# A masked feed-forward kernel: last two batches kept on chip, weight rounding dealt out anew, every second unit in three passes

## The reference, cut to what matters

```python
def cond(x, session_ids, channel_counts, seq_lens, W_sess, b_sess, W2, b2):   # x: 32 x 128 x 2048
    xm = x * cmask[:, :, None]
    h = gelu(einsum('bct,bch->bht', xm, W_sess[session_ids]) + b)             # 256 hidden rows
    out = einsum('bht,hs->bst', h, W2) + b2[None, :, None]
    return out * tmask[:, None, :]

def ffn(o, weight, bias):                                                     # weight: 2048 x 2048
    w_scale = 448 / max(abs(weight));   w_q = (weight * w_scale) as fp8 e4m3
    o_scale = 57344 / max(abs(o));      o_q = (o * o_scale) as fp8 e5m2
    return einsum('bsk,nk->bsn', o_q, w_q) / o_scale / w_scale + bias

result = x + ffn(cond(x, ...), weight, bias)
```

## Time and profile before

| | |
|---|---|
| median of 3 runs | 832.85 us (832.84 to 832.87) |
| profiled execution | 833.1 us, span of its records 831.3 us |
| TensorE products busy | 825.8 us, 99% of the span |
| VectorE busy | 479.5 us, 58% |
| ScalarE busy | 345.9 us, 42% |
| GpSimd busy | 511.8 us, 62% |
| first stage, passage, second stage | up to about 381 us, to about 391 us, to the end |
| granted clock of TensorE | 1.00 in every stretch |

### The profile page before, as it was taken

The page is one execution under the profiler, slowest core; times in us unless marked ns, Lnnn a source line. Parts: engine busy times, 40 slices in busy tenths (PEclk is TensorE's granted clock), DMA queues, the critical chain, the costliest instruction groups (busy, mean ns, idle before and its releaser), DMA issues.

```text
span 831.3 us, 10181 instructions
## 1 busy us (share of the span) xinstructions
PE 825.8 (99%) x3568; PEld 479.9 (58%) x3568; DVE 479.5 (58%) x499; ACT 345.9 (42%) x372; POOL 511.8 (62%) x238
## 2 busy tenths in 40 slices
PE   9999999999999999999999999999999999999998
PEld 5777777776767676765444444444444444444444
DVE  6989889788888888888553232323232323232322
ACT  7999999988888888973100000000000000000000
POOL 2899999899999999995983242424242423232322
PEclk9999999999999999999999999999999999999999
DMA  7988999877777877657974868686868686868682
GB/s 258 322 321 321 367 339 353 301 285 296 284 289 303 305 267 301 253 187 246 298 295 119 282 214 282 210 285 212 280 213 280 214 283 214 279 213 282 215 248 107
DMA packets 75008, 220.77 MB, mean 266 GB/s; under 512 B 37594, under 2 KB 40930, under 8 KB 55778
## 3 DMA queue, kind: packets, MB, share of 16 engines
q1 hardware_dynamic: 74080, 219.30, 74.5%
q10 hardware_dynamic: 898, 1.09, 0.4%
HBM read 143.04 MB, written 69.21 MB: 255 GB/s over the span
## 4 chain that ended last, share of the span: by engine, by line
PE 99%; issue 0%; POOL 0%; DVE 0%; ACT 0%; POOLq 0%
PE ps_h L1071 53%; PE ps_h L980 22%; PE ps_o L995 11%; PE ps_o L1011 8%; PE ps_o L1007 4%; PE ps_o L934 1%; PE ps_h L1047 0%; PE ps_o L1071 0%; PE ps_o L980 0%; PE ps_o L1065 0%; POOL time L518 0%; PE ps_o L940 0%; PE ps_h L1052 0%; DVE o_and_max L881 0%; ACT x_sb L702 0%
## 5 line engine op out<-in xcount | busy, mean ns | idle before, releaser
L1071 PE MATMUL ps_h<-wqT,x_sb 128*128 128x512 bf16 x1920 | 413.7, 378 | 0.2 <-ACT x_sb L702 0.2
L1071 PEld LDWEIGHTS ps_h<-wqT,x_sb 128*128 128x128 fp8e5 x1920 | 187.7, 98 | 224.4 <-ACT x_sb L702 0.3
L528 POOL TENSOR_TENSOR xl<-x_sb,xh 128x1024 fp32r<-128x1024 f32 x62 | 149.5, 2411 | 16.3 <-ACT xh L607 16.3
L980 PE MATMUL ps_h<-xh,whl 128*128 128x512 f32 x508 | 150.3, 417 | 0.4
L569 POOL TENSOR_TENSOR x_sb<-x_sb,bias_sb 128x2048 f32<-128x2048 f32 (+1 forms) x15 | 66.7, 4447 | 131.7 <-DMA x_sb<-in_x 131.7
L569 POOL TENSOR_TENSOR h<-h,bias_sb 128x2048 f32<-128x2048 f32 (+1 forms) x15 | 66.7, 4443 | 122.7 <-DMA h<-in_x 122.7
L881 DVE SCALAR_TENSOR_TENSOR o_and_max<-ps_h,scales,h 128x512 f32<-128x512 f32 (+1 forms) x59 | 44.0, 746 | 136.2 <-PE ps_h L1071 136.2
L881 DVE SCALAR_TENSOR_TENSOR o_and_max<-ps_h,scales,x_sb 128x512 f32<-128x512 f32 x59 | 44.2, 750 | 133.4 <-PE ps_h L1071 133.4
L980 PEld LDWEIGHTS ps_h<-xh,whl 128*128 128x128 f32 x508 | 94.2, 188 | 42.0 <-issue 21.7
L765 DVE SCALAR_TENSOR_TENSOR o_and_max<-ps_o,b_sb,steps 128x1024 f32<-128x1024 f32 (+1 forms) x65 | 82.2, 1264 | 29.0 <-PE ps_o L1011 27.1
L755 DVE TENSOR_TENSOR hl<-ps_h,hh 128x1024 fp32r<-128x1024 f32 x63 | 76.8, 1219 | 13.4 <-ACT ps_h L614 13.3
(11 more groups left out here) (101 smaller groups left out, 657.2 us busy)
## 6 DMA issues: line engine op xcount, KB each, us to landing
x_sb<-in_x SPq DMA_DIRECT2D x44, 1024.0 KB, 5.7
masked_out<-o_and_max SPq DMA_DIRECT2D x32, 1024.0 KB, 6.8
o_in<-masked_out SPq DMA_DIRECT2D x32, 1024.0 KB, 8.9
...
```

Of the source, the lines that this page charges most:

```text
L528: pool.tensor_tensor(xl[:, u % 2, :], x_cols(u), xh[:, u % 2, :].bitcast(fp32), ALU.subtract)\
L980: mm = nc.tensor.matmul(to[:, cols], whl[:, b % SLOTS_W, rows], xs[:, u % 2, cols], start=(k == 0), stop=(k == 2))
L1071: mm = nc.tensor.matmul(bank, q[:, k // 2, :, k % 2], wq[:, n, k, cols], start=(k == 0), stop=(k == KT - 1))
```

## The change

It has four parts.

1. *Three-pass units.* `SPLIT_H1` grows from units 2 to 26 to units 2 to 28. From 29 to 61 every second unit (`SPLIT_BEHIND`, 17 units) takes three passes in another way: ScalarE writes `hh1_behind` and the gelu in place in PSUM, and VectorE subtracts them straight from PSUM (`split_h1_behind`). `hidden(u+1, 1)` then waits for that subtraction.
2. *Rounding the weight.* ScalarE writes the absolute value, scaled up, in two-byte form into `wc`; GpSimd bounds that from both sides in place (`lift_constant`), VectorE scales the chunk and adds the constant in one instruction (`add_round_at`), GpSimd subtracts the constant as before. `QUANT` grows by two, so ten chunks are late, not eight.
3. *Order on VectorE.* `add_round_at` stands behind `split_h_rest(u + 1)`, where the exponents stood ahead of it. In units of `SPLIT_BEHIND` `scan_o` goes behind it too.
4. *Kept batches.* The last two batches of o and of x stay in SBUF. The second stage begins with them (`KEPT`, `batch_at`) and goes on with batches 0 to 29. Converted and turned data move to the space of `h1`.

```diff
-    SPLIT_H1 = [u for u in range(2, 27)]
+    SPLIT_H1 = [u for u in range(2, 29)]
+    SPLIT_BEHIND = [u for u in range(29, UNITS - 2, 2)]
...
-    QUANT = SCANS + 2
+    QUANT = SCANS + 4
...
-    QUAD = 4
+    QUAD, KEPT = 4, 2
...
+        hh1_behind = sb_at("hh1_behind", [P, 2, UNIT], fp32r, h1_at)
+        hl1_behind = sb_at("hl1_behind", [P, UNIT], fp32r, raw_at)
...
-        xs = x_sb[:, 1, :]
+        xs = h1[:, :, :].rearrange("p a n -> p (a n)")
...
-        x2 = (x_sb[:, 0, :], h1[:, :, :].rearrange("p a n -> p (a n)"))
+        x2 = (x_sb[:, 0, :], x_sb[:, 1, :])
...
+            def lift_constant(i):
+
+                c = wc[:, i % 2, 0:chunk_cols(i)]
+                pool.wait_ge(w_raised, i + 1)
+                pool.tensor_scalar(c, c, 2.0 * E4M3_MAX * ROUND_AT, 1.5 * E4M3_MIN_NORMAL * ROUND_AT, ALU.min, ALU.max)\
+                    .then_inc(w_floored, 1)
+
             def round_chunk(i):
 
                 v, c = ws[:, i % 2, 0:chunk_cols(i)], wc[:, i % 2, 0:chunk_cols(i)]
-                pool.wait_ge(w_round_ready, i + 1)
-                pool.tensor_tensor(v, v, c, ALU.add).then_inc(w_added, 1)
                 pool.wait_ge(w_added, i + 1)
...
                 if 0 <= u - QUANT - 1 < EARLY_CHUNKS:
                     round_chunk(u - QUANT - 1)
+                if 0 <= u - QUANT < EARLY_CHUNKS + 1:
+                    lift_constant(u - QUANT)
...
-            pool.wait_ge(x2_loaded[0], 16)
             add_bias(x2[0], FRONT)
-            for i in late[0:2]:
+            round_chunk(late[0])
+            lift_constant(late[1])
+            pool.wait_ge(xl_ready, UNITS)
+            add_bias(x2[1], FRONT)
+            lift_constant(late[2])
+            pool.wait_ge(q_ready, CUTS)
...
+                if u in SPLIT_BEHIND:
+                    act.activation(hh1_behind[:, u % 2, :], ps_h[:, 1, :], ACT.Gelu, bias=hbias[:, 1, b:b + 1])
+                    act.activation(ps_h[:, 1, :], ps_h[:, 1, :], ACT.Gelu, bias=hbias[:, 1, b:b + 1])\
+                       .then_inc(h1_gelu, 1)
+                    return
...
-                act.activation(ws[:, i % 2, 0:chunk_cols(i)], wt[:, at:at + chunk_cols(i)], ACT.Copy, scale=w_scale)\
-                   .then_inc(w_scaled, 1)
+                act.activation(wc[:, i % 2, 0:chunk_cols(i)], wt[:, at:at + chunk_cols(i)], ACT.Abs, scale=w_up)\
+                   .then_inc(w_raised, 1)
...
+            def split_h1_behind(u):
+
+                dve.wait_ge(h1_gelu, u + 1)
+                if u == SPLIT_BEHIND[0]:
+                    dve.wait_ge(wl_later, DIRECT - UPB)
+                dve.tensor_tensor(hl1_behind[:, :], ps_h[:, 1, :], hh1_behind[:, u % 2, :].bitcast(fp32), ALU.subtract)\
+                   .then_inc(hl1_behind_ready, 1)
...
+            def add_round_at(i):
+
+                c, at = wc[:, i % 2, 0:chunk_cols(i)], i % 3 * CHUNK
+                dve.wait_ge(w_floored, i + 1)
+                dve.scalar_tensor_tensor(ws[:, i % 2, 0:chunk_cols(i)], wt[:, at:at + chunk_cols(i)], w_scale, c,
+                                         ALU.mult, ALU.add).then_inc(w_added, 1)
...
+                    if u - 1 in SPLIT_BEHIND:
+                        pe.wait_ge(hl1_behind_ready, SPLIT_BEHIND.index(u - 1) + 1)
...
-                if u == UNITS - 4:
-
-                    sp.wait_ge(xl_ready, UNITS - 2)
-                    load_x_again(0, 0, FRONT)
...
-            sp.wait_ge(o_masked, UNITS + 1)
-            store_o(B - 1)
...
             for k in range(CUTS):
-                quantize(0, 1, k == 0, CUT[k])
+                quantize_kept(0, CUT[k])
```

More of the change, by code:

```diff
@@ L71, in adaln_ffn @@
     QUANT_AT = [2, 5, 10]
-    CHUNK_BEHIND = range(4, 12)
+    CHUNK_BEHIND = (2, 4, 5, 6, 7, 8)
     TAIL = [slice(BANK * (NC - 1), BANK * NC - BANK // 2), slice(BANK * NC - BANK // 2, BANK * NC)]
@@ L443, in _ @@
             turn(1)
-            for r in range(2):
-                sp.wait_ge(o_stored[r], 2 * 16)
-                load_o(2 + r, r)
-            for r in range(2):
-                sp.dma_start(x2_more[r][:, FRONT], x[2 + r, :, FRONT]).then_inc(x2_more_loaded[r], 16)
+            load_x_more(1)
             for b in range(2):
@@ L572, in _ @@
             pool.wait_ge(bias_loaded, 16)
-            pool.wait_ge(x2_loaded[0], 16)
             add_bias(x2[0], FRONT)
-            for i in late[0:2]:
+            round_chunk(late[0])
[4 more added lines that the diff above has]
+            pool.wait_ge(q_ready, CUTS)
+            for b in range(KEPT):
+                pool.tensor_tensor(x3[:, b, :], x2[b][:, FRONT.stop:F], bias_sb[:, FRONT.stop:F], ALU.add).then_inc(x3_ready, 1)
+            for i in late[1:7]:
                 round_chunk(i)
-            pool.wait_ge(x2_loaded[1], 16)
-            add_bias(x2[1], FRONT)
-            for i in late[2:6]:
-                round_chunk(i)
+                lift_constant(i + 2)
             pool.wait_ge(x2_more_loaded[0], 16)
             add_bias(x2_more[0], FRONT)
-            for i in late[6:]:
+            for i in late[7:]:
                 round_chunk(i)
+                if i + 2 < CHUNKS:
+                    lift_constant(i + 2)
             pool.wait_ge(x2_more_loaded[1], 16)
@@ L587, in _ @@
             pool.wait_ge(x3_loaded, 16)
-            for b in range(QUAD):
+            for b in range(KEPT, QUAD):
                 pool.tensor_tensor(x3[:, b, :], x3[:, b, :], bias_sb[:, FRONT.stop:F], ALU.add).then_inc(x3_ready, 1)
@@ L627, in scale_chunk @@
                 if i == 0:
[L628 removed]
+                    act.wait_ge(w_scale_ready, 2)
                 if i >= 2:
@@ L704, in _ @@
                    .then_inc(q_widened, 1)
-            for i in range(EARLY_CHUNKS + 2, CHUNKS):
-                scale_chunk(i)
-                if UNITS - QUANT + 2 <= i + 3 < CHUNKS:
-                    act.wait_ge(w_scaled, i + 1)
+            for i in range(EARLY_CHUNKS + 1, CHUNKS - 1):
+                if i > EARLY_CHUNKS + 1:
+                    scale_chunk(i + 1)
+                if i + 3 < CHUNKS:
+                    act.wait_ge(w_added, i + 1)
                     at = i % 3 * CHUNK
@@ L873, in _ @@
             for i in late[1:4]:
-                exponents(i)
-                round_at(i)
+                add_round_at(i)
             dve.wait_ge(scale_step, 7)
@@ L902, in _ @@
                        .then_inc(y_ready, 1)
-                if y in CHUNK_BEHIND and 4 + CHUNK_BEHIND.index(y) < len(late):
+                if y in CHUNK_BEHIND:
                     i = late[4 + CHUNK_BEHIND.index(y)]
-                    exponents(i)
-                    round_at(i)
+                    add_round_at(i)
             def step2(i, last):
@@ L1007, in project1 @@
                             mm = nc.tensor.matmul(ps_o[:, u % 2, cols], w[:, :], hs[:, u % 2, cols],
+                                                  start=False, stop=(j == 2))
+                elif u in SPLIT_BEHIND:
+                    for j, (w, hs) in enumerate(((w2l1, hh1_behind[:, u % 2, :]), (w2h1, hh1_behind[:, u % 2, :]),
+                                                 (w2h1, hl1_behind))):
+                        for cols in halves:
+                            mm = nc.tensor.matmul(ps_o[:, u % 2, cols], w[:, :], hs[:, cols],
                                                   start=False, stop=(j == 2))
```

122 lines of the change are left out of this document (58 added, 64 removed).

## The result

The changed kernel takes 837.53 us (836.76 to 837.67), the kernel before 832.85 (832.65 to 833.25) beside it: a ratio of 1.0054, 95% interval 1.0042 to 1.0065. It is slower by 4.7 us, where 0.6 less was forecast, and outside the range. The profiled executions have spans of 835.7 and 831.3 us, 4.4 apart.

The account below looks back on a forecast made before the run. The prediction took TensorE to bound both stages. Its terms, -0.4 for units 27 and 28, -2.2 for the 17 units and +2.0 for the passage, summed to -0.6 us, giving 832.2 us, with a range from 829.6 to 837.

Parts of the forecast that it names:

- What bounds the kernel: Both stages: TensorE bounds them, with three engines close behind in the first; only its work or waits move the end.
- Units 27 and 28, -0.4: First stage: these two units become three-pass, each 0.20 us shorter, a gain of 0.4 us.
- The 17 behind units, -2.2: First stage, every second unit from 29 to 61: 0.20 us gained less 0.07 of waiting each, 2.2 us in all.
- It fits by 0.09 us. I take 0 here: First stage: the loop shared by GpSimd and VectorE takes 5.73 us a unit, under TensorE's 5.82, so costs 0.
- GpSimd becomes the bound: Rival, first stage: a lifting of 1.0 us or more sets the pace; 834.5 at 1.0, 843.0 at 1.25; chance 0.18.
- busy without a gap: First stage, sign that GpSimd binds: GpSimd never idles, with the lifting's row over 0.93 us.
- VectorE's split late by 0.07, or 0.28: First stage: TensorE waits 0.07 us for the new split; rival with the whole 0.28, 834 to 835.9, chance 0.10.
- the second case: Rival, first stage and passage: three passes gain the full 3.4 us, passage costs 0.9; 830.0 us, chance 0.30.
- ScalarE, 0: First stage: ScalarE's one more activation in each of the 17 units costs 0, with thin cover.
- The passage, +2.0: Between the stages: VectorE's scale-and-add waits for GpSimd's bias add, costing 2.0 us, with 0.9 and 2.2 as ends.
- Miss each other narrowly: Between the stages: second bias add ends near 385.3, a further lifting at 386.2, just before the conversions at 386.25.
- Kept batches, 0: Second stage: dropping two stores and two loads of o, and the loads of x, gains 0, transfers being already hidden.

Follow-up runs that it names:

- no_behind: The changed kernel with its 17 half-and-half units (29, 31 ... 61) back to the plain float32 product: 836.9 us, ratio 1.0055.
- behind_28: The kernel before plus VectorE's new split in 17 units, and units 27 and 28 three-pass with the weight chunks kept in place: 832.64 us, ratio 0.9997.
- no_lift: The changed kernel with GpSimd lifting 2 of each chunk's 768 columns, the others left out: 832.41 us, ratio 0.9995.
- behind_alone: The kernel before with only VectorE's new split in 17 units (29 to 61) taken over from the change: 830.97 us, ratio 0.9976.
- split_first: The changed kernel with VectorE's new split ahead of the mask of the unit before in the 17 units: 837.64 us, ratio 1.006.
- passage: The changed kernel with chunk 33's scale-and-add behind the first conversions, both bias adds ahead, ScalarE's scaling of a late chunk behind its copies: 840.34 us, ratio 1.0092.
- bias_later: The changed kernel with GpSimd doing the subtract of chunk 33 before the first bias add: 840.44 us, ratio 1.0095.
- warmer: The changed kernel with 18 idle TensorE products instead of 8 while the scale is worked out: 836.58 us, ratio 1.0048.

## Why the prediction was wrong

**What bounds the kernel** was read rightly: 4.17 of the 4.42 us lie ahead of the unbroken products, which start at 395.65 instead of 391.48.

**Units 27 and 28, -0.4.** This held. no_behind has them without the 17 behind units: its gelu of half 0 starts at 161.58 ahead of them and, seven units on, at 201.89, where before it was 161.87 and 202.59, so 0.41 is gained. It needs the chunks to start two units later, as they do in the change: behind_28, where they don't, loses by it.

**The 17 behind units, -2.2.** This step failed. A pair takes 11.90 instead of 11.78 us, so the 17 cost 17 x 0.12 = 2.0 us instead of giving 2.2. (With the -0.4 that makes +1.6; the first stage shows +1.13, since this execution is 0.36 ahead already at 161.51, in front of unit 27.) The sentence that failed is the one on GpSimd and VectorE: "It fits by 0.09 us. I take 0 here". The loop was seen, and summed to 5.73; it measures 5.95, half of the 11.90. The parts: split of x 2.41, remainder of the scale-and-add 0.82 (forecast 0.85), subtract 1.67 (1.66), lifting 0.83 (0.84). Each part was right to 0.03 us. What was wrong is the seams. I took one handoff of 0.05 and then took 0.08 off for overlap, two rows overlapping by some 0.04 each as GpSimd's subtract and the split behind it do in the earlier trace rows. Around the lifting nothing overlaps: the seams of the rows above are 0.07 (242.78 to 242.85), 0.08 (244.52 to 244.60) and 0.08 (245.43 to 245.51), +0.23 instead of -0.03. The earlier trace rows had such a seam too, 0.08 from the add to the subtract, and I passed over it. That makes 2.41 + 0.82 + 1.67 + 0.83 + 0.23 = 5.96, over the 5.82 that was needed by 0.14, where I thought it fitted by 0.09. no_lift shows the closure from one side (0.64 out of the loop, stage at -2.24), behind_alone from the other (no loop, -1.98 at the start of the products).

**The rival "GpSimd becomes the bound"** had the right mechanism, with a chance of 0.18, and was tied to the wrong quantity. Its condition was a lifting of 1.0 us or more; the lifting was 0.83, inside the forecast, and the case came true all the same. The condition should have been the loop against 5.82, with 0.09 of room against an error in three seams. That GpSimd is then "busy without a gap", as the prediction said, is wrong too: it idles 0.89 a unit for VectorE, and VectorE's time goes into a long row. On the size of the lifting, the Trainium skill, "GPSIMD Engine Reference", section 3.1, led to estimates of 0.66 and 1.15; the 0.83 lies between.

**VectorE's split late by 0.07, or 0.28.** 0.33 us at 251.29. But most of this is the loop's delay, seen where TensorE meets it: waits of this size are gone in behind_alone and, but for one, in no_lift, and split_first only moved them. Two rivals, 0.28 and the loop, gave nearly the same row, and only taking one away told them apart. The split's own cost is the 0.10 a pair of no_lift, near the 0.07 of the forecast; the handoff behind it, taken as 0.05, is 0.10 to 0.12. No run got the full 3.4 us of the second case.

**ScalarE, 0** held: behind_alone has the same extra activation, at 58.9 busy of 60 us, and TensorE doesn't wait.

**The passage, +2.0.** +2.26: mechanism and place right (2.42 us long, held by the bias add). "Miss each other narrowly" was right: the bias add ended 0.7 us ahead of the conversions, the lifting ran 0.2 us into them, and they took 3.00 us, as in the runs where neither was there (passage). bias_later shows what a hit costs.

**The clock was left out.** The forecast had 0 behind the first conversion. The longer passage left TensorE without work for 2.3 us, and the next products ran at down to half clock: +1.03 us. warmer takes 0.96 of it away.

**Kept batches, 0.** Nothing contradicts it, but it wasn't taken out by itself. TensorE is busy 100 of 100 us behind, as before.

**Still open** is the rest of no_behind: its passage at +2.99 and +1.36 behind. The growing scale-and-adds explain that it is over +2.26; what share of the second is the clock wasn't measured by itself. And no version with the short passage and timely late chunks was run.
